# Attention's maxima in rounds of two halves of queries, taken from neighbouring head groups

## The reference, cut to what matters

```python
qkv = x @ Wqkv                                   # x: (16, 1024, 256)
Q, K = _apply_rope(Q, cos, sin), _apply_rope(K, cos, sin)
scores = jnp.einsum('bhqd,bhkd->bhqk', Q, K) / math.sqrt(Dh)
scores = jnp.where(causal, scores, jnp.finfo(scores.dtype).min)
attn = jax.nn.softmax(scores, axis=-1)
y = jnp.einsum('bhqk,bhkd->bhqd', attn, V)
...
return y @ Wproj
```

## Time and profile before

| | us |
|---|---|
| median of 3 runs | 10044.25 |
| the profiled execution, as timed | 10042.81 |
| its span, first to last instruction | 10040.9 |
| a turn | 616 to 619 |
| of it attention (last turn, 9421.8 to 9563.3) | 141.5 |

### The profile page before, as it was taken

One profiled execution on the slowest core, in us unless ns is written; L12 is line 12 of the kernel. 1 busy time (PEld: TensorE's weight loads), 2 busy tenths in 40 slices (PEclk: granted clock), 3 DMA queues, 4 the chain that ended last, 5 costly groups with the idle time before them and its releaser, 6 DMA issues. The chain is left out here.

```text
span 10040.9 us, 98208 instructions
## 1 busy us (share of the span) xinstructions
PE 7867.1 (78%) x31796; PEld 3819.5 (38%) x31796; DVE 7696.5 (77%) x11686; ACT 4309.5 (43%) x8247; POOL 4340.3 (43%) x2663
## 2 busy tenths in 40 slices
PE   5787787787877878787887878778787787877877
PEld 2343343433434334343343433434343343432434
DVE  4787877779687686876868768787787877878777
ACT  2534535354442543525435254353534535345352
POOL 1451714518154171542716336262361724517145
PEclk8898988989889898888989889898898988989889
DMA  3010020200202002020020200102011020100202
GB/s 76 1 38 15 5 48 1 51 1 5 48 0 51 1 9 44 0 51 1 12 40 0 51 1 21 32 0 52 1 28 25 0 52 1 38 15 5 48 0 51
DMA packets 260295, 229.91 MB, mean 23 GB/s; under 512 B 22051, under 2 KB 232739, under 8 KB 259635
## 3 DMA queue, kind: packets, MB, share of 16 engines
q1 hardware_dynamic: 259782, 223.48, 11.6%
HBM read 151.60 MB, written 70.25 MB: 22 GB/s over the span
## 5 line engine op out<-in xcount | busy, mean ns | idle before, releaser
L625 POOL TENSOR_TENSOR arena<-arena 128x1024 f32<-128x1024 f32 x1024 | 2434.3, 2387 | 1330.6 <-DVE arena L1007 879.0
L766 ACT ACTIVATE PS<-arena,Aneg 128x512 f32<-128x512 f32 x2048 | 1410.6, 691 | 1627.2 <-DVE XNT L1047 883.2
L690 ACT ACTIVATE arena<-PS 128x512 f32<-128x512 f32 (+3 forms) x3072 | 1286.8, 509 | 867.0 <-PE PS L1213 861.8
L914 DVE TENSOR_REDUCE pm<-PS 128x1 f32<-128x512 f32 (+3 forms) x1728 | 1050.6, 661 | 336.5 <-PE PS L1192 234.9
L1327 PE MATMUL PS<-XNT,identf 128*128 128x512 f32 x2048 | 1012.1, 618 | 320.0 <-POOL XNT L608 320.0
L587 POOL TENSOR_SCALAR_AFFINE_SELECT arena<-arena 128x512 f32<-128x512 f32 x512 | 328.2, 641 | 2114.5 <-ACT arena L690 2114.5
L1189 PE MATMUL PS<-arena 96*128 96x512 bf16 (+3 forms) x3072 | 1098.0, 382 | 178.8 <-PEq L1411 87.3
L1327 PE MATMUL PS<-arena,identf 128*128 128x512 f32 x2048 | 1025.5, 624 | 161.8 <-DVE arena L1023 161.8
L1213 PE MATMUL PS<-arena 99*128 99x512 bf16 (+3 forms) x3072 | 891.8, 331 | 5.4
L1150 PE MATMUL PS<-identf,arena 128*128 128x128 f32 x1280 | 284.1, 387 | 776.0 <-POOL arena L577 664.6
L1312 PE MATMUL PS<-arena,sel 96*128 96x512 bf16 x1664 | 513.4, 391 | 389.2 <-DVE arena L1023 319.7
(11 more groups left out here) (140 smaller groups left out, 13240.7 us busy)
## 6 DMA issues: line engine op xcount, KB each, us to landing
pieces_scratch<-arena SPq DMA_DIRECT2D x816, 64.0 KB
arena<-pieces_scratch SPq DMA_DIRECT2D x34, 768.0 KB
arena<-pieces_scratch SPq DMA_DIRECT2D x51, 512.0 KB
arena<-pieces_scratch SPq DMA_DIRECT2D x17, 1536.0 KB
arena<-in_x SPq DMA_DIRECT2D x17, 1024.0 KB, 5.6
U<-in_x SPq DMA_DIRECT2D x17, 1024.0 KB, 5.6
arena<-pieces_scratch SPq DMA_DIRECT2D x17, 1024.0 KB
out<-X SPq DMA_DIRECT2D x64, 256.0 KB, 8.3
```

The lines of the kernel that those rows point to most:

```text
L625: nc.gpsimd.tensor_tensor(DB[:, n % 2], DTU[:, j, half(th)].unsqueeze(1).to_broadcast([P, SP2, TH]), BB[:, SP2 * sg:SP2 * (sg + 1), :], AL ...
L690: A(PT[s % len(PT)][:, hh, 0:w], bank(t_bank(n))[:, 0:w], ACT.Exp, scale=DH ** -0.5)\
L766: A(bank(da_bank(m)), DT[:, j, half(th)], ACT.Exp, scale=Aneg[:, j, SP2 * sg + ss:SP2 * sg + ss + 1]).then_inc(S("dA"), 1)
L914: V_.tensor_reduce(out=dst, in_=bank(r % 3)[:, 0:share * w].rearrange("p (h w) -> p h w", h=share), op=ALU.max, axis=AX.X, negate=True).th ...
```

## The change

The eight pairs of head group and half of queries become `TASKS`, in the same order as before. Maxima go in five rounds in place of four: round 0 is the first half of group 0; rounds 1 to 3 are the second half of one group with the first half of the next; round 4 is the second half of group 3. Score units keep their order (0 to 191); rounds end at u = 16, 64, 112, 160 and 192. The exponential's units of a task start no sooner than 14 units behind the end of its round, one a unit (`T_AT`). Each round has its transpose and its split; its rows go to SyncE by task, three transfers each, with a semaphore for either half (`mrow0`, `mrow1`). `QS` is laid out by half of the queries, so the stack of the queries is loaded in two halves too, with six transfers in place of three. `pm` is cleared once, ahead of the loop.

```diff
-S_UNITS = [(hh, i, c) for i in range(NT) for c in range(1 + (i * P) // TH) for hh in range(HG)]
-NS1 = len(S_UNITS)
+NHT = NT // NTH
+TASKS = [(g, qc) for g in range(NG) for qc in range(NTH)]
+ROUND_OF = [(k + 1) // 2 for k in range(len(TASKS))]
+NROUND = ROUND_OF[-1] + 1
+S_SEQ = [(k, hh, i, c) for k, (g, qc) in enumerate(TASKS) for i in range(qc * NHT, (qc + 1) * NHT)
+         for c in range(1 + qc) for hh in range(HG)]
+NU = len(S_SEQ)
+S_END = [sum(ROUND_OF[k] <= n for k, _, _, _ in S_SEQ) for n in range(NROUND)]
+T_STEPS = [(k, j) for k, (g, qc) in enumerate(TASKS) for j in range((qc + 1) * TH // P)]
+NST = len(T_STEPS)
+NTU = NST * HG
+LAG = 14
+T_AT = []
+for _n in range(NTU):
+    T_AT.append(max(T_AT[-1] + 1 if T_AT else 0, S_END[ROUND_OF[T_STEPS[_n // HG][0]]] + LAG))
+T_OF = {u: n for n, u in enumerate(T_AT)}
 def s_width(i, c):
...
-        QS = view(0, 8192, BF16).rearrange("p (h t) -> p h t", h=H)
+        QS = view(0, 8192, BF16).rearrange("p (q h t) -> p q h t", q=NTH, h=H)
...
+        last_of = [last_step(k) for k in range(len(TASKS))]
+        pv_at = [T_AT[HG * s + HG - 1] + 2 * HG for s in range(NST)]
+        pv_of = {u: s for s, u in enumerate(pv_at)}
+        evac_at = {pv_at[s]: k for k, s in enumerate(last_of)}
+        ot_at = {pv_at[s] + HG: k for k, s in enumerate(last_of)}
+        y_at = {pv_at[s] + HG + 2: k for k, s in enumerate(last_of)}
...
+        mt_at = {S_END[r] + 2: r for r in range(NROUND)}
+        pieces_at = {S_END[r] + 3: r for r in range(NROUND)}
...
-                sp.dma_start(((QS, KS)[qk])[row:row + n, heads, cols],
+                sp.dma_start(KS[row:row + n, heads, cols] if qk else QS[row:row + n, cols.start // TH, heads, :],
                              pcd[qk, heads, lo:hi, :, cols].rearrange("h n d t -> (n d) h t"))\
...
-        N_STACK = 1 + 3 * len(RUNS[0])
+        N_STACK = 1 + 4 * len(RUNS[0])
...
-            stack(sp, 0, ALL, slice(0, T))
+            for qc in range(NTH):
+                stack(sp, 0, ALL, half(qc))
...
-            for g in range(NG):
-                if g:
-                    sp.wait_ge(S("mrow"), 16 * PIECES * g)
-                sp.wait_ge(S("mpiece"), g + 1)
-                for n in range(PIECES):
-                    sp.dma_start(QS[SR + n:SR + n + 1, g * HG:(g + 1) * HG, :], mp[:, g % 2, n, :])\
-                      .then_inc(S("mrow"), 16)
+            for r in range(NROUND):
+                if r:
+                    sp.wait_ge(S("mrow0"), 16 * PIECES * r)
+                if r > 1:
+                    sp.wait_ge(S("mrow1"), 16 * PIECES * (r - 1))
+                sp.wait_ge(S("mpiece"), r + 1)
+                for k, (g, qc) in enumerate(TASKS):
+                    if ROUND_OF[k] == r:
+                        part = slice((1 - qc) * HG * NHT, (2 - qc) * HG * NHT)
+                        for n in range(PIECES):
+                            sp.dma_start(QS[SR + n:SR + n + 1, qc, g * HG:(g + 1) * HG, :], mp[part, r % 2, n, :])\
+                              .then_inc(S(("mrow0", "mrow1")[qc]), 16)
...
-                    g, hh, i, c, w, r, share = s_unit(u)
-                    if g >= 2 and u % NS1 == 0:
-                        dve.wait_ge(S("mT"), g - 1)
+                    k, g, hh, i, c, w, b, share = s_unit(u)
+                    r = ROUND_OF[k]
+                    if r >= 2 and u == S_END[r - 1]:
+                        dve.wait_ge(S("mT"), r - 1)
                     if hh % share == share - 1:
                         heads = slice(hh + 1 - share, hh + 1)
-                        dst = px[:, g % 2, heads, i - TH // P] if c else pm[:, g % 2, heads, i]
-                        dve.wait_ge(S("S"), r + 1)
-                        V_.tensor_reduce(out=dst, in_=bank(r % 3)[:, 0:share * w].rearrange("p (h w) -> p h w", h=share),
+                        dst = (px[:, r % 2] if c else pm[:, r % 2, 1 - TASKS[k][1]])[:, heads, i % NHT]
+                        dve.wait_ge(S("S"), b + 1)
+                        V_.tensor_reduce(out=dst, in_=bank(b % 3)[:, 0:share * w].rearrange("p (h w) -> p h w", h=share),
                                          op=ALU.max, axis=AX.X, negate=True).then_inc(S("red"), 1)
-                    if u % NS1 == NS1 - 1:
-                        dve.wait_ge(S("red"), NRED * (g + 1))
-                        V_.tensor_tensor(pm[:, g % 2, :, TH // P:], pm[:, g % 2, :, TH // P:], px[:, g % 2],
-                                         ALU.min).then_inc(S("pmax"), 1)
-                if u >= NS1 and u % NS1 == 3 and u // NS1 <= NG:
-                    g = u // NS1 - 1
+                    if r and u == S_END[r] - 1 - (r < NROUND - 1) * HG * NHT:
+                        dve.wait_ge(S("red"), sum(S_LAST[:u + 1]))
+                        V_.tensor_tensor(pm[:, r % 2, 0], pm[:, r % 2, 0], px[:, r % 2], ALU.min).then_inc(S("pmax"), 1)
+                if u in pieces_at:
+                    r = pieces_at[u]
                     mt = PS[0:HG * NT, 7, 0:P]
-                    dve.wait_ge(S("mT"), g + 1)
-                    if g >= 2:
-                        dve.wait_ge(S("mrow"), 16 * PIECES * (g - 1))
-                    own.link(V_.tensor_copy(mp[:, g % 2, 0, :], mt))
-                    own.link(V_.tensor_tensor(mr[:, :], mt, mp[:, g % 2, 0, :], ALU.subtract))
-                    own.link(V_.tensor_copy(mp[:, g % 2, 1, :], mr[:, :]))
-                    V_.tensor_tensor(mp[:, g % 2, 2, :], mr[:, :], mp[:, g % 2, 1, :], ALU.subtract)\
+                    dve.wait_ge(S("mT"), r + 1)
+                    if r >= 2:
+                        dve.wait_ge(S("mrow0"), 16 * PIECES * (r - 1))
+                    if r >= 3:
+                        dve.wait_ge(S("mrow1"), 16 * PIECES * (r - 2))
...
-                if u >= NS1 and u % NS1 == 2 and u // NS1 <= NG:
-                    g = u // NS1 - 1
-                    pe.wait_ge(S("pmax"), g + 1)
+                if u in mt_at:
+                    r = mt_at[u]
+                    pe.wait_ge(S("red"), sum(S_LAST[:S_END[r]]))
+                    if r:
+                        pe.wait_ge(S("pmax"), r)
                     if turned:
                         pe.wait_ge(S("y"), turned)
-                    maxima = g + 1
-                    nc.tensor.transpose(PS[0:HG * NT, 7, 0:P], pm[:, g % 2].rearrange("p h i -> p (h i)"), identf[:, :])\
+                    maxima = r + 1
+                    nc.tensor.transpose(PS[0:HG * NT, 7, 0:P], pm[:, r % 2].rearrange("p q h i -> p (q h i)"), identf[:, :])\
                         .then_inc(S("mT"), 1)
-                n = u - NS1 - LAG
-                if 0 <= n < NS2 * NG:
-                    s, hh, g, qc, j, q0, w = t_unit(n)
+                n = T_OF.get(u)
+                if n is not None:
+                    s, hh, k, g, qc, j, q0, w = t_unit(n)
                     h = g * HG + hh
-                    if n % NS2 == 0:
-                        pe.wait_ge(S("mrow"), 16 * PIECES * (g + 1))
+                    if hh == 0 and j == 0:
+                        pe.wait_ge(S(("mrow0", "mrow1")[qc]), 16 * PIECES * (g + 1))
                     if T6 <= n < T6 + 3:
-                        pe.wait_ge(S("red"), NRED * NG)
+                        pe.wait_ge(S("red"), NRED)
                     elif n >= 3:
                         pe.wait_ge(S("expd"), n - 2 if n < T6 else n - 5)
                     MM(bank(t_bank(n))[:, 0:w], KS[0:SR + PIECES, h, tile(j)],
-                       QS[0:SR + PIECES, h, q0:q0 + w], start=True, stop=True).then_inc(S("ST"), 1)
-                if u >= pv_at[0] and (u - pv_at[0]) % HG == 0 and (u - pv_at[0]) // HG < NST * NG:
-                    s = (u - pv_at[0]) // HG
-                    _, _, g, qc, j, q0, w = t_unit(s * HG)
-                    oc = g * NTH + qc
+                       QS[0:SR + PIECES, qc, h, TH - w:TH], start=True, stop=True).then_inc(S("ST"), 1)
```

More of the change, by code:

```diff
@@ L72, in s_share, with last_step @@
     return min(HG, TH // s_width(i, c))
-S_LAST = [hh % s_share(i, c) == s_share(i, c) - 1 for hh, i, c in S_UNITS]
+S_LAST = [hh % s_share(i, c) == s_share(i, c) - 1 for _, hh, i, c in S_SEQ]
 NRED = sum(S_LAST)
[L78 to L88, removed]
+def last_step(k):
+    return max(s for s, (m, _) in enumerate(T_STEPS) if m == k)
 def build(nc, x_in, wqkv_in, wproj_in, ipw_in, convw_in, convb_in, xpw_in, dtw_in, dtb_in, alog_in, d_in, opw_in,
@@ L342, in build, with s_unit @@
         ov = out.rearrange("b (i p) c -> b p i c", p=P)
[L343 to L347, removed]
-        U_END = max(y_at) + 1
[L349 to L355, removed]
+        last_of = [last_step(k) for k in range(len(TASKS))]
[4 more added lines that the diff above has]
+        y_at = {pv_at[s] + HG + 2: k for k, s in enumerate(last_of)}
+        U_END = max(y_at) + 1
+        mt_at = {S_END[r] + 2: r for r in range(NROUND)}
+        pieces_at = {S_END[r] + 3: r for r in range(NROUND)}
+        def s_unit(u):
+            k, hh, i, c = S_SEQ[u]
```

(33 more changed lines are left out.)

20 lines of the change are left out of this document (14 added, 6 removed), and 2 rows, old and new, of the table names.

## The result

The changed kernel takes 10068.62 us (median of 12 runs, 10060.23 to 10076.23), the kernel before 10043.56 beside it (12 runs): a ratio of 1.0025, 95% interval 1.0017 to 1.0034. It is slower, by 25 us; the forecast was 10003, with 10054 as its upper end. One of before's 12 executions took 10776.6 us, far above the others, and the ratio leaves it out.

The account below looks back on a forecast made before the run. No engine bounds the kernel throughout: VectorE limits the maxima, TensorE most exponentials, SyncE's 2.7 us wait each turn's end. From 10042.8 us, -43 - 5 + 7 gives 10001.8, 10003 as a median; range 9965 to 10054.

Parts of the forecast that it names:

- Term 4: Query-stack transfers at each turn's end: 1 KB runs reach 175 GB/s, SyncE's 2.7 us wait vanishes; -43 and -5 us.
- rival (b): Query-stack transfers: short runs are no faster, the wait stays and only attention counts; 10051 us, chance 0.12.
- rival (c): Query-stack transfers at the turn's end: short runs cost more per byte, slower kernel; 10113 us at 116 GB/s, chance 0.07.
- Term 1: End of attention: 16 more units cover the wait for the last small transfers; 0.07 us a turn, 1 us in all.
- Term 2: Attention up to unit 78: 17th exponential's scores come at 37.7 us, 0.4 us later than before.
- Term 3: Attention behind unit 78: second exponential start at the slow clock costs 1.6 us; products and transposes moved ahead save 1.5.
- Terms 2 and 3 together: Attention up to and behind unit 78: +0.5 us a turn, from -1.7 to +2.5.
- Rival (d): First 16 exponentials: TensorE's clock doesn't rise there, 4.7 us a turn more; 10078 us, chance 0.07.
- Rival (e): Between the two groups of exponentials: the clock stays up, the second slow start's 1.6 us goes; 9977 us, chance 0.06.

Follow-up runs that it names:

- before_split: Kernel before with the query stack (six transfers, not three) and the rows of the maxima in two halves, four rounds kept: 10036.86 us, 0.9993 of before.
- after_warm_gap: Changed kernel with one unused TensorE product more a unit in units 48 to 77: 10041.88 us, 0.9999 of before.
- after_late: Changed kernel with the first 16 exponentials back at units 62 to 77, as before: 9997.85 us, 0.9952 of before.
- late_drain: after_late with TensorE waiting at unit 50 until VectorE has reduced all of group 0: 10015.48 us, 0.9973 of before.
- late_warm: after_late with unused TensorE products in units 12 to 61: 9995.08 us, 0.9956 of before.
- late_warm_quant: late_warm with 154 more unused products a turn and a TensorE wait ahead of each of the two quantised products: 10032.80 us, 0.9990 of before.

## Why the prediction was wrong, by its own steps

**Term 4, the step that failed.** It was to give 48 us, and gave 0.34 a turn, some 5: 43 of the 66 us between forecast and result. "It is the same kind of transfer" was false: the two windows differed in the run's size, in the rows of the part and in the place in the queue, and I read the whole difference as the run's. The rows for the test were in the trace of before, since the queries' own 32 rows, in 2 KB runs, go at 187. That was rival (b), at 0.12. The Trainium skill's rule (page "DMA: Bandwidth & Descriptors", section "Why small descriptors are slow (HBM only)"), by which I had worked out 10068, meets the measured time by chance: no part here became slower with 1 KB by more than 187 to 179, and the stack lands sooner, not later.

That a us of this wait is a us of the turn nearly holds for what lies behind VectorE's last instruction: before_split takes 0.84 out of the wait and 0.71 out of that part. But the turn does not change, because VectorE ends 0.66 later; the low stretch right behind attention, in 15 turns and not 11, is some 0.3 of it, and the rest stays open. The bound of "about 137 GB/s" in rival (c) doesn't come out of the prediction's own numbers either: with 23.5 us and 2.7 of wait, each lost us counts below some 151.

**Term 1** was to give -0.07 a turn; from the 145th exponential to the end it is 25.64 before and 25.54 after: right. The change does shorten what it says, and there was nothing to shorten.

**Term 2** was to give +0.4, measured +1.13. The wait for the small transfers holds (scores at 12.8 behind the first reduction, forecast 12.3 to 13.0). In the last turn the 17th's scores come at 38.3 and not 37.6: VectorE is busy for 36.7 of it (27.11 and 9.56 in the first two stretches) and idle for 1.6, forecast 36.1 and 1.5. So the losses were sized right, though the slow start lasted 4.9 us and not 3.3, and what was too good is that TensorE runs two reductions (1.2 us) ahead: with VectorE's sum of 37.3, it was about one ahead.

**Term 3** was to give +1.6 - 1.5 = +0.1; measured +2.03 - 1.15 = +0.88. The mechanism is the forecast one, shown by after_warm_gap, which takes it away. The size was off: the second slow start was taken at 3.3 us, and is 5.3 in the mean of the turns, 3.4 to 6.7. I had three cases of a first start in the earlier trace rows, all short, and none of a start behind a stretch as in the gap.

**Terms 2 and 3 together** were to give +0.5 (-1.7 to +2.5), measured +2.03: inside, near the edge. The profiled execution's sum with what was measured: 10042.8 + 16 x (2.03 + 0.42 - 0.34) = 10076.6, against its 10075.27; it is one of the longer of the 12 runs, whose median is 10068.62.

**Rival (d)** didn't come: the clock rose in the first 16 exponentials. **Rival (e)** didn't: it fell again between the groups. **Rival (c)** has the time but not the mechanism.

**What I hadn't counted at all.** The rounds move the first join behind the point where TensorE would wait for it. after_late shows what the rounds are worth with the exponentials left where they were, 45 us, of which late_drain ties 18 to that wait; the other 27 are not divided. I counted the extra round as work in a VectorE-bound place and asked nothing of its order. The early exponentials spend this gain and 25 us more.

## What to carry to other kernels

Work that is pulled ahead of a stretch where TensorE mostly waits can leave the clock to fall twice; look at the granted clock where the first TensorE-bound stretch begins, and prefer to start that stretch once, with the clock up. Here 50 unused products a turn in front of it gave 0.48%, as much as a better order did, and the two didn't add. What a stretch at the slow clock costs hangs on whether another engine waits for TensorE in it, so compare single turns and not sums. Before two DMA windows are compared for one property, find the packets of one part in each, so that everything else is equal.

## What the hardware showed that I had not expected

- The rate of a stacking transfer hangs on its rows: 48 rows 131 to 137 GB/s when not first in the queue, 32 rows 177 to 188, with 1 KB and 2 KB runs alike; 16 rows 126 with 2 KB and 162 with 1 KB. Whether it is their number or their place (0 to 47, 48 to 79, 80 to 95) is not shown.
- Nine such issues hold SyncE for 18.32 us, six for 7.70: three more cost 10.6 us, not 3.9. Here nothing waited for it.
- TensorE stayed at the slow clock for up to 6.7 us in which it was busy almost without a break (in the last turn 6.78 of the 6.80 us from 9490.90), and one wait of about 0.4 us in the maxima moved the rise by 3 us.
- With 154 more products in TensorE's loop (2185 a turn for late_warm's 2031) its closing branch took 3.3 to 3.9 us and not 0.36. The page of late_warm, then of late_warm_quant, has these instruction transfers (number, MB, share):

```profile
q8 instruction: 272, 4.46, 0.2%
```

```profile
q8 instruction: 304, 4.98, 0.2%
```

Two more a turn. The Trainium skill, page "Runtime: NRT & Kernel Launch", section "Instruction fetch mechanics", says that a taken branch whose target isn't among the instructions held forces a fetch. The longer branch here looks like that, but late_warm's loop, 7% shorter, took 0.36, and no run here shows from which length on it comes.
